# 16-head attention kernel: who turns the heads into fp16 high and low parts (GpSimd alone, or ScalarE and VectorE between the steps)

## The reference, cut to what matters

```python
q = (lat @ Wq).reshape(b, q_len, 16, 64).transpose(0, 2, 1, 3)       # q_len = 2048
k = (kv_input @ Wk).reshape(b, f + q_len, 16, 64).transpose(0, 2, 1, 3)
v = (kv_input @ Wv).reshape(b, f + q_len, 16, 64).transpose(0, 2, 1, 3)
sim = jnp.einsum('bhqd,bhfd->bhqf', q * 0.125, k)
alphas = jax.nn.softmax(jnp.where(kv_mask, sim, -jnp.inf), axis=-1)
out = jnp.einsum('bhqf,bhfd->bhqd', alphas, v)
return out.transpose(0, 2, 1, 3).reshape(b, q_len, 1024) @ Wo
x = x + jnp.tanh(g_xattn[0]) * attention(...)
```

## Time and profile before

| what | us |
|---|---|
| median of 3 runs | 3161.93 (3158.17 to 3164.2) |
| the profiled execution | 3158.64 |
| its span in the profile | 3156.8 |
| the eight pairs of heads | about 74 to 1788 of the span |

### The profile page before, as it was taken

The page is one execution under the profiler, slowest core; times in us unless marked ns, Lnnn a source line. Parts: engine busy times, 40 slices in busy tenths (PEclk is TensorE's granted clock), DMA queues, the critical chain, the costliest instruction groups (busy, mean ns, idle before and its releaser), DMA issues. The chain is left out here.

```text
span 3156.8 us, 71255 instructions
## 1 busy us (share of the span) xinstructions
PE 2921.6 (93%) x29442; PEld 1445.3 (46%) x29442; DVE 2231.5 (71%) x2703; ACT 1941.4 (61%) x2643; POOL 504.8 (16%) x569
## 2 busy tenths in 40 slices
PE   5999999999999999999999797899996997989988
PEld 3444444444444444444445355222224665557655
DVE  6888888888878888888878876100006886778866
ACT  5665655656656656556556523799994775247741
POOL 0000000000001000000000010200002773247710
PEclk9999999999999999999999899999998999999999
DMA  2000000000000000000000002111101001000000
GB/s 80 8 2 7 3 2 7 3 2 9 2 7 4 2 7 3 2 2 3 2 2 2 32 1 88 62 28 28 37 19 52 15 8 40 20 14 21 1 1 27
DMA packets 30037, 51.69 MB, mean 16 GB/s; under 512 B 6072, under 2 KB 22539, under 8 KB 28555
## 3 DMA queue, kind: packets, MB, share of 16 engines
q1 hardware_dynamic: 29706, 46.91, 4.7%
HBM read 41.04 MB, written 5.83 MB: 15 GB/s over the span
## 5 line engine op out<-in xcount | busy, mean ns | idle before, releaser
L767 ACT ACTIVATE a_probs<-PS 128x1024 f32<-128x1024 f32 x928 | 949.2, 1024 | 589.2 <-PE PS L521 582.5
L534 PE MATMUL PS<-a_probs,a_V 64*64 64x512 f32 x7424 | 974.3, 590 | 5.8 <-DVE a_heads_outT L954 5.3
L998 DVE TENSOR_TENSOR a_prob_sums<-a_prob_sums,a_probs 128x1024 f32<-128x1024 f32 x512 | 628.4, 1227 | 125.8 <-ACT a_probs L767 102.7
L995 DVE SCALAR_TENSOR_TENSOR a_prob_sums<-a_probs,a_valid,a_prob_sums 128x1024 f32<-128x1024 f32 x384 | 498.5, 1298 | 70.5 <-ACT a_probs L767 60.3
L1816 ACT ACTIVATE c_probs<-PS 128x1024 f32<-128x1024 f32 (+1 forms) x416 | 382.4, 1085 | 8.7 <-PE PS L1735 7.0
L521 PE MATMUL PS<-a_Q_hi,a_K_hi 64*64 64x512 f16 x3712 | 380.5, 381 | 4.4 <-ACT a_probs L767 4.4
L521 PE MATMUL PS<-a_Q_hi,a_K_lo 64*64 64x512 f16 x3712 | 378.1, 377 | 2.9 <-issue 2.9
L521 PE MATMUL PS<-a_Q_lo,a_K_hi 64*64 64x512 f16 x3712 | 378.7, 377 | 1.9 <-issue 1.9
L534 PEld LDWEIGHTS PS<-a_probs,a_V 64*64 64x64 f32 x7424 | 286.8, 133 | 168.5 <-issue 21.0
L67 POOL CAST a_heads_hi<-a_heads_outT 128x512 f16<-128x512 f32 x31 | 49.6, 1601 | 1468.8 <-DVE a_heads_outT L967 1468.8
L521 PEld LDWEIGHTS PS<-a_Q_hi,a_K_hi 64*64 64x64 f16 x3712 | 117.0, 106 | 273.4 <-issue 267.8
(11 more groups left out here) (346 smaller groups left out, 4413.5 us busy)
## 6 DMA issues: line engine op xcount, KB each, us to landing
c_Qop<-q_part SPq DMA_DIRECT2D x96, 64.0 KB, 2.3
c_Kop<-k_part SPq DMA_DIRECT2D x96, 50.0 KB, 2.0
d_raw<-in_l1f_w_dram SPq DMA_DIRECT2D x18, 256.0 KB, 3.2
d_tables<-in_rotary_dram SPq DMA_DIRECT2D x2, 2048.0 KB, 10.7
X<-in_x_dram SPq DMA_DIRECT2D x2, 1024.0 KB, 10.0
out_dram<-X SPq DMA_DIRECT2D x4, 512.0 KB, 3.5
c_cT<-in_ctxT_dram SPq DMA_DIRECT2D x1, 1601.0 KB, 6.5
a_probs<-in_ctx_dram SPq DMA_DIRECT2D x3, 512.0 KB, 5.5
```

The lines of the kernel that those rows point to most:

```text
L534: last = nc.tensor.matmul(m.PS[64 * h:64 * h + 64, PVB + g, :], V[e][rows, s, 64 * h:64 * h + 64], probs[n % 4][rows, h * BANK:(h + 1) * B ...
L767: nc.scalar.activation(probs[n % 4][:], m.PS[:, b0:b0 + 2, :].rearrange("p b c -> p (b c)"), ACT.Exp).then_inc(exped, 1)
L995: nc.vector.scalar_tensor_tensor(out=sums, in0=new, scalar=valid[:, s:s + 1], in1=sums, op0=ALU.mult, op1=ALU.add).then_inc(summed, 1)
L998: nc.vector.tensor_tensor(sums, sums, new, ALU.add).then_inc(summed, 1)
```

## The change

GpSimd keeps only the output weight. The high part of chunk c is now an ACTIVATE Copy on ScalarE (`take_heads_hi`), placed behind the exponential of the step after VectorE's multiplication: behind exponentials 39, 68 and 97 for chunks 0 to 2 and behind exponential 9 of the next pair for chunk 3. It waits for `heads_done`, which that multiplication raises, and for the earlier `mixed`. The low part is a TENSOR_TENSOR on VectorE (`take_heads_lo`), one step later still: behind accumulations 40, 69, 98 and 10. Chunk 3 of the last pair stays as it was. The semaphores and their counts are the same ones.

```diff
@@ -322,6 +322,8 @@
+        HEADS_HI_AT = {n + 1: c for n, (c, j) in INVERT_AT.items() if j == PARTS}
@@ -444,19 +446,9 @@ (GpSimd)
-                def split_heads(i, c):
-
-                    n, cols = i * CHUNKS + c, slice(c * BANK, (c + 1) * BANK)
-                    pool.wait_ge(heads_done, n + 1)
-                    take_hi(nc.gpsimd, heads_hi[:, cols], heads_outT[:, cols]).then_inc(heads_hi_done, 1)
-                    pool.wait_ge(heads_hi_done, n + 1)
-                    take_lo(nc.gpsimd, heads_lo[:, cols], heads_outT[:, cols], heads_hi[:, cols]).then_inc(heads_split, 1)
-
                 pool.wait_ge(ones_done, 3)
                 for i in range(PAIRS):
                     split_wo(i)
-                    for c in range(CHUNKS if i < PAIRS - 1 else CHUNKS - 1):
-                        split_heads(i, c)
@@ -757,6 +749,14 @@ (ScalarE)
+                def take_heads_hi(i, c):
+
+                    cols = slice(c * BANK, (c + 1) * BANK)
+                    act.wait_ge(heads_done, i * CHUNKS + c + 1)
+                    if i:
+                        act.wait_ge(mixed, i * MIXES)
+                    nc.scalar.activation(heads_hi[:, cols], heads_outT[:, cols], ACT.Copy).then_inc(heads_hi_done, 1)
@@ -768,6 +768,12 @@
                         if n in TAKE_AT:
                             take_half(i, TAKE_AT[n])
+                        if n in HEADS_HI_AT:
+                            c = HEADS_HI_AT[n]
+                            if c < CHUNKS - 1:
+                                take_heads_hi(i, c)
+                            elif not first:
+                                take_heads_hi(i - 1, c)
@@ -966,6 +972,12 @@ (VectorE)
+                def take_heads_lo(i, c):
+
+                    cols = slice(c * BANK, (c + 1) * BANK)
+                    dve.wait_ge(heads_hi_done, i * CHUNKS + c + 1)
+                    take_lo(nc.vector, heads_lo[:, cols], heads_outT[:, cols], heads_hi[:, cols]).then_inc(heads_split, 1)
@@ -1023,6 +1035,12 @@
+                        if n - 1 in HEADS_HI_AT:
+                            c = HEADS_HI_AT[n - 1]
+                            if c < CHUNKS - 1:
+                                take_heads_lo(i, c)
+                            elif not first:
+                                take_heads_lo(i - 1, c)
```

## The result

The changed kernel takes **3174.3 us** in the median of 6 runs (3170.62 to 3177.25), the kernel before 3161.48 us in 6 runs (3158.17 to 3167.92). The ratio is 1.0038, 95% interval [1.0025, 1.0051]: 0.38% slower. The forecast was 3175.4 us.

A forecast was written before the change was run, and what follows sets the result against it. TensorE was taken to bound the pairs; 7 x 1.35 + 3 x 1.36 = 13.5 us of stalls, all else at nothing, on 3161.9 gave 3175.4 us. Its own range was 3170 to 3181 (66%), the whole range 3164 to 3188.

The forecast's parts named there:

- The bound, and who is held: Inside pairs TensorE sets the pace, 1.51 us a step; the cast holds ScalarE 2.26 us for VectorE's late multiplication.
- bare place: Place with no TensorE unit between cast and next scores; TensorE loses 1.35 us (1.36 in the last pair).
- square: ScalarE's square of a 128x512 SBUF tile, taken as the cast's length: 0.62 us, adding 0.52 to the queue.
- table of units: The code's placing of TensorE units: chunk 3 of pairs 0 to 6 and chunks 0 to 2 of the last pair pay.
- covers: TensorE's own projection hides the delay in pairs 0 to 6: 0.48 us left at chunk 0, 0.52 at chunk 1.
- VectorE and GpSimd at nothing: Low part adds 0.6 us to VectorE's queue, relief from GpSimd frees 0.88 per chunk; both counted as costing nothing.
- upper bound of the cast: GpSimd's cast of the same tile, 1.60 us: +16 us, from 1.0 more at 10 places and 0.5 at 14.
- Covered places break open: Rival, 11%: cast or wake-up up to 1 us longer, 24 places pay; up to 3191 us, likelier 3183.
- given back: Rival, 10%: the loss is regained in a later TensorE wait or never made; no change, 3162 us.
- Faster: Rival, 6%: VectorE's accumulations beside GpSimd held the exponentials, so their relief counts; 8 us gained, 3154 us.
- The clock drops too: Rival, 7%: TensorE's stalls lower its clock at all ten places, 1.65 us each; 3192 us.
- argument from the pauses of 1.56 and 2.67 us: TensorE's clock stayed 1.00 after 1.56 us idle, fell to 0.50 after 2.67; a 1.35 us stall is shorter than both.

The follow-up runs named there:

- wait-only kernel: Kernel before, nothing moved, but ScalarE waits for the multiplication where the changed kernel casts; 3171.27 us, 1.0027 of the kernel before.
- Bare only: Changed kernel with only chunk 3 of pairs 0 to 6 and chunks 0 to 2 of the last pair moved; 3175.95 us, 1.0039 of the kernel before.
- covered only: Changed kernel with only the 21 chunks moved that have a unit behind them, the other 10 left on GpSimd; 3162.77 us, 0.9998 of the kernel before.
- triple cast: Changed kernel with two further casts of the same tile, which nobody reads, ahead of each real one; 3200.34 us, 1.0121 of the kernel before.
- versions two and three later: Changed kernel with cast and low part moved to behind exponential M-step + 2 or + 3 instead of + 1; 3165.71 and 3163.33 us, both 1.0005.
- high part only: Changed kernel with the low parts back on GpSimd, ScalarE still casting the high parts; 3177.51 us, 1.0041 of the kernel before.
- double cast: Changed kernel with one further cast of the same tile, which nobody reads, ahead of each real one; 3181.46 us, 1.0062 of the kernel before.
- two with only one sort of these stalls: Changed kernel with only chunks 0 to 2 of the last pair moved, 3166.18 us; or only chunk 3 of pairs 0 to 6, 3171.92 us.
- one sooner: Changed kernel with the cast one exponential earlier, behind exponential M-step instead of + 1; 3232.18 us, 1.0226 of the kernel before.

## Why the prediction was right

**The bound, and who is held.** TensorE sets the pace in the pairs, and the cast holds ScalarE until VectorE's late multiplication is done. The profile after shows it (2.3 us, 31 times), and the wait-only kernel shows that the wait alone does most of it: with none of these casts on ScalarE 0.83 of the 1.35 us at each place remain. The other 0.52 are the cast's, and they too count only behind the wait: two and three steps later the same casts cost nothing that can be told.

**The price of a bare place.** 1.35 us forecast, 1.35 to 1.36 measured ten times. Of its terms the cast takes 0.63 us where 0.62 was taken from the square, and adds 0.54 against 0.52 (0.52 by the difference of the wait-only kernel). The slope holds as well: 1.87 us with two casts and 2.39 with three.

**Which places pay.** Ten of 31, by the table of units. Bare only and covered only divide the loss into all and nothing, and the triple cast measures the covers, 0.48 and 0.51 us, by breaking them open (1.04 less 0.56 and 0.53). The forecast was 0.48 and 0.52.

**VectorE and GpSimd at nothing.** The accumulations did shrink, but by less than the 0.88 us per chunk that the prediction read at one place: 498.5 - 480.5 = 18.0 us in all, 0.58 per chunk. This term was not in the sum. The line of the earlier trace rows now reads

```profile
L1007 DVE SCALAR_TENSOR_TENSOR a_prob_sums<-a_probs,a_valid,a_prob_sums x384: 1182/1280/1287, 79.4 to 1779.4; 128x1024 f32<-128x1024 f32 x192
```

and no longer reaches 2004 ns. That the relief is worth nothing is shown by the versions two and three later, which have all of it and no stall, and take the time of the kernel before. The exclusive lock that the Trainium skill states (page "SBUF — State Buffer", section "Who interferes with whom") is seen here as a slowing of at most 0.72 us for one accumulation (2004 ns against 1283), not as a whole GpSimd instruction's length. That the two do interfere, the rows confirm: without GpSimd's splitting no accumulation takes more than 1287 ns.

**The sum.** 13.5 us forecast; 13.4 in the pairs of the profiled execution, 12.8 between the medians. That the total comes so close is partly luck. The ten places give 13.5 us by themselves, but the low clock in the last pair adds 1.7 us that the forecast had not, and the scatter of the other distances happens to take it back; what bears the account are the ten distances. The upper bound of the cast is a little off, too: 1.0 us at 10 places and 0.5 at 14 are 17 us, not 16.

**The rivals.** "Covered places break open" and "given back" did not happen. "Faster" has fallen with the two later versions. "The clock drops too" did not happen behind the ten stalls of 1.35 us, but the mechanism is real: it was not seen right behind stalls of 1.87 us (none of ten), behind those of 2.39 us it was three of ten, and behind those of 2.86 us nine of 17. The price of 1.65 us for each was about right (1.40 to 1.79 measured). The argument from the pauses of 1.56 and 2.67 us gave the right side for the ten stalls, but it took the clock to go by the length of the pause alone, and the last section shows a pause of 1.77 us that is followed by either clock. That low stretch of the changed kernel is no sign against the forecast's path, since the pause ahead of it is in the kernel before as well, but the forecast had no term for it.

## What to carry to other kernels

Before a wait is put on an engine that idles a third of the time, read at that place how late the producer is and how soon the bounding engine wants the instruction queued behind; the price is producer's end + moved work + next instruction + wake-up, less the time at which it is wanted, and only where that is positive. Covers are local: the same line of code cost 1.35 us at ten places and nothing at 21. One step of position removed the loss, while one in the other direction made it more than five times as large. Freeing GpSimd, which nobody waited for here, gained nothing, even though it also relieved VectorE.

## What the runs showed of the hardware

The granted clock does not fall at a fixed length of pause. Pauses of the same length at the same place (1.77 us of idle time at the end of chunk 1 in the last pair) were followed by a clock of 1.00 in the kernel before and of 0.50 for 3.4 us in the changed one. It cost 1.7 us: from scores 57 to scores 64 the changed kernel takes 14.92 us, the kernel before 13.23. TensorE's rows behind the two pauses and the windows behind them, before and changed:

```profile
1698.25 1.09 PE L534 MATMUL PS<-a_probs,a_V 64*64 64x512 f32 x8 [1.77 <-DVE a_heads_outT L954]
```

```profile
1698.30:1701.50 3.20, 3.20 (x44) 1.82 (x48) 1.26 (x2) 1.02 (x1) 0.00 (x0) 1.00 0.02 5
```

```profile
1709.33 1.26 PE L526 MATMUL PS<-a_probs,a_V 64*64 64x512 f32 x8 [1.77 <-DVE a_heads_outT L960]
```

```profile
1710.30:1713.50 3.20, 3.20 (x28) 1.66 (x24) 0.54 (x1) 1.02 (x1) 0.00 (x0) 0.50 0.02 5
```

The clock was low there in four kernels (changed, bare only, high part only, double cast), all of which stall 1.35 us or more both at chunk 3 and in the last pair; the seven distances from scores 57 to 64 are 14.92 us in each of them. It was not low in the two with only one sort of these stalls, nor in the wait-only kernel with its stalls of 0.83 us, and neither in the triple cast and the one sooner, which have both sorts and longer. What decides stays open. Stalls of 2.39 and 2.86 us were likewise followed by it only at some of the places, all alike in the code.

GpSimd's subtraction took 2.0 us beside VectorE's accumulations in the kernel before (median of 31) and 1.47 us in the high-part-only kernel, while the worst accumulation took 2004 and 1694 ns. So the duration of neither is a constant there. That it depends on where the two overlap is likely but was not tested.
